# A deformable convolution and a ternary convolution block on one core: the work in front of the loop in another order, with image 0's offsets summed and replicated ahead of its pixels' low parts and their store

## What is computed

```python
x = x + L0(gn(x))    # deformable 3x3 convolution, 128 -> 128 channels
x = x + L1(gn(x))    # two ternary 3x3 convolutions with batch norm, relu(out1 + out2)

# L0, in short
om = conv2d(x, w_off) + b_off                  # 27 channels: 9 row offsets, 9 column offsets, 9 masks
mask = sigmoid(m)
sampled = four corners of x at (base + tap + offset), bilinear, times mask
out = einsum('bckhw,ock->bohw', sampled, weight) + bias
out = group_norm(out, 16 groups) * gamma + beta
```

## Time and profile before

| | us |
|---|---|
| median of 3 runs | 272.83 |
| lowest, highest | 272.41, 274.51 |
| the profiled execution | 272.33 |
| its span in the trace | 270.6 |
| TensorE busy in the span | 244.2 |
| VectorE | 213.6 |
| ScalarE | 171.9 |
| GpSimd | 166.3 |

### The profile page before, as it was taken

The page is one execution under the profiler, slowest core; times in us unless marked ns, Lnnn a source line. Parts: engine busy times, 40 slices in busy tenths (PEclk is TensorE's granted clock), DMA queues, the critical chain, the costliest instruction groups (busy, mean ns, idle before and its releaser), DMA issues.

```text
span 270.6 us, 5607 instructions
## 1 busy us (share of the span) xinstructions
PE 244.2 (90%) x1960; PEld 210.8 (78%) x1960; DVE 213.6 (79%) x473; ACT 171.9 (64%) x364; POOL 166.3 (61%) x217
## 2 busy tenths in 40 slices
PE   6989998999999899998998999899999999999800
PEld 6867666899988799897998888899987776777600
DVE  5599556989888999559979789985588787699493
ACT  2488756989779978877799778757216406630140
POOL 8000899999668788777668987486900601936051
PEclk9999999999999999999999999999999999999965
DMA  7925686544444422333323334300000000000016
GB/s 216 378 69 186 208 263 239 164 146 135 133 140 135 127 95 75 110 114 108 111 79 105 96 131 132 103 30 2 0 0 0 2 1 0 0 0 2 5 54 261
DMA packets 25593, 28.13 MB, mean 104 GB/s; under 512 B 2509, under 2 KB 23613, under 8 KB 25560
## 3 DMA queue, kind: packets, MB, share of 16 engines
q1 hardware_dynamic: 24912, 25.95, 29.3%
q10 hardware_dynamic: 648, 1.76, 1.8%
HBM read 19.87 MB, written 6.78 MB: 99 GB/s over the span
## 4 chain that ended last, share of the span: by engine, by line
PE 64%; DVE 22%; ACT 8%; issue 2%; DMA 1%; DVEq 0%
PE PS L949 13%; PE PS L855 6%; PE PS L741 5%; PE PS L808 5%; PE PS L857 5%; PE PS L856 5%; PE PS L837 5%; DVE slo L1556 5%; PE PS L984 4%; PE PS L838 4%; PE PS L839 4%; DVE vlo L1567 3%; DVE st L1455 3%; ACT vhi L1165 3%; PE PS L767 2%
## 5 line engine op out<-in xcount | busy, mean ns | idle before, releaser
L581 POOL TENSOR_TENSOR vt<-rowm,hat 128x1026 f32<-128x1026 f32 x36 | 70.8, 1966 | 25.9 <-PE PS L817 24.1
L1567 DVE TENSOR_TENSOR vlo<-PS,vhi 128x576 fp32r<-128x576 f32 (+2 forms) x88 | 50.1, 590 | 17.5 <-ACT vhi L1165 17.2
L1165 ACT ACTIVATE vhi<-PS 128x576 fp32r<-128x576 f32 (+2 forms) x88 | 43.8, 523 | 19.1 <-PE PS L839 19.0
L1556 DVE TENSOR_TENSOR slo<-PS,shi 114x512 fp32r<-114x512 f32 (+1 forms) x68 | 43.2, 675 | 6.3 <-ACT shi L1153 6.0
L855 PE MATMUL PS<-vhi,wdhi 128*128 128x256 f32 x144 | 43.4, 301 | 0.8 <-ACT xb L1172 0.7
L837 PE MATMUL PS<-shi,patch 114*128 114x288 f32 (+1 forms) x136 | 42.0, 309 | 1.0 <-DVE vlo L1567 0.6
L857 PE MATMUL PS<-vhi,wdlo 128*128 128x256 f32 x144 | 40.5, 281 | 0.0
L856 PE MATMUL PS<-vlo,wdhi 128*128 128x256 f32 x144 | 40.4, 281 | 0.0
L838 PE MATMUL PS<-slo,patch 114*128 114x288 f32 (+1 forms) x136 | 40.2, 296 | 0.0
L839 PE MATMUL PS<-shi,patch 114*128 114x288 f32 (+1 forms) x136 | 40.0, 294 | 0.0
L1153 ACT ACTIVATE shi<-PS 114x512 fp32r<-114x512 f32 (+1 forms) x68 | 36.7, 592 | 4.9 <-PE PS L808 4.4
(11 more groups left out here) (217 smaller groups left out, 518.0 us busy)
## 6 DMA issues: line engine op xcount, KB each, us to landing
patch<-xt SPq DMA_DIRECT2D x136, 114.0 KB
xt<-xtv SPq DMA_DIRECT2D x4, 1024.0 KB, 6.2
xs<-in_x SPq DMA_DIRECT2D x3, 512.0 KB, 7.5
wraw<-in_L_conv_w SPq DMA_DIRECT2D x2, 576.0 KB, 9.5
out<-xb SPq DMA_DIRECT2D x4, 256.0 KB, 2.6
wd_raw<-in_L_conv_weight ACTq DMA_DIRECT2D x1, 576.0 KB, 6.9
xs<-in_x SPq DMA_DIRECT2D x2, 256.0 KB, 4.1
omr<-omr SPq DMA_DIRECT2D x8, 64.0 KB, 4.5
```

The source lines that it names most:

```text
L581: g.tensor_tensor(vt[:, n % 2, :, :].rearrange("p t (r j) -> p t r j", r=WR), rowm[:, n % 2, :, :].unsqueeze(3).to_broadcast([P, TAPS, WR, ...
L1165: last = a.activation(places(vhi), src, ACT.Copy)
L1556: d.tensor_tensor(lo, src, hi, ALU.subtract).then_inc(slo_ok, 1 if pairs(n) == 2 else 3)
L1567: last = d.tensor_tensor(places(vlo), src, places(vhi), ALU.subtract)
```

## The change

The change moves steps of the work in front of the loop, on every engine:

- SyncE issues `replicate(0)` ahead of `store_pixels(0)`.
- VectorE does half of image 2's statistics earlier, `deformable_lo(2)` ahead of the second `deviation`, then `scale_shift(GN0, 2)`, `offsets(0)`, `offsets(1)` and only then `pixels_lo(0)`. It also makes `xlo` of image 3, behind `offsets(3)` and ahead of `pixels_lo(3)`; `low_parts(3)` on GpSimd is gone.
- ScalarE does `tail(0)` and `tail(1)` ahead of `whole(GN0, 1)`.
- TensorE takes the group mean of images 2 and 3 after the last of six matmuls of `offset_part(1, 0, 0)` instead of after the first, `group_square(GN0, 2)` behind `turn_offsets(0)`, and `turn_image(1)` ahead of `offset_part(1, 0, 1)`.
- The six matmuls of `keep_going` at the start (128 columns, on the identity, after GpSimd made it) give way to nine of 512 columns on a tile of zeros, which can start once VectorE has written the zeros.

```diff
@@ sync
+            replicate(0)
             store_pixels(0)
-            replicate(0)
             sp.wait_ge(zpad_out, 16 * (B + 1))
             store_pixels(1)
@@ gpsimd
-                if n == -4:
-                    low_parts(3)
@@ tensor
-            pe.wait_ge(consts, 1)
-            keep_going(6)
+            zeros = woffT[:, :, :, :].rearrange("p l x c -> p (l x c)")
+            pe.wait_ge(zeroed, 4)
+            for _ in range(9):
+                t.matmul(PS[0:STACK, 5, :], zeros[:, 0:STACK], zeros[:, 0:BIG], start=True, stop=True)
...
             SUMS = {(0, 0, 0): ((group_mean, 1, (2, 0)),), (0, 1, 0): ((group_square, 1, (0, 0)),),
-                    (1, 0, 0): ((group_mean, 2, (0, 0)), (group_square, 2, (2, 1)))}
+                    (1, 0, 0): ((group_mean, 2, (2, 1)),)}
...
             turn_offsets(0)
+            group_square(GN0, 2)
+            turn_image(1)
             offset_part(1, 0, 1)
-            turn_image(1)
@@ scalar
             heads(GN0, 1)
-            whole(GN0, 1)
             tail(0)
             tail(1)
+            whole(GN0, 1)
@@ vector
             image_stats(GN0, 1)
+            dve.wait_ge(x_in[2], 16)
+            half_stats(GN0, 2, 0)
             deviation(GN0, 1)
...
-            dve.wait_ge(x_in[2], 16)
-            image_stats(GN0, 2, last=False)
+            image_stats(GN0, 2, last=False, halves=(1,))
             deformable_lo(0)
             dve.wait_ge(x_in[3], 16)
             image_stats(GN0, 3)
             deformable_lo(1)
+            dve.wait_ge(pads, 11)
+            deformable_lo(2)
             deviation(GN0, 2)
             tails(GN0, 1)
...
-            dve.wait_ge(pads, 11)
-            deformable_lo(2)
-            pixels_lo(0)
+            scale_shift(GN0, 2)
             offsets(0)
             offsets(1)
-            scale_shift(GN0, 2)
+            pixels_lo(0)
             whole_late(2)
...
             offsets(3)
+            dve.wait_ge(xhi_ok, B)
+            dve.wait_ge(xn_late, 2)
+            d.tensor_tensor(inner(xlo, B - 1), square(plain(B - 1)), inner(xhi, B - 1), ALU.subtract).then_inc(xlo_last, 1)
             pixels_lo(3)
```

More of the change, by code:

```diff
@@ L181, in build @@
             sem(n) for n in ("gn_in", "gn_mean", "gn_dev", "gn_msq", "gn_var", "gn_std", "gn_ok"))
-        xhi_top, xhi_ok, xlo_ok, xlo_pool, xlo_first, xn_ok, xn_late = (
-            sem(n) for n in ("xhi_top", "xhi_ok", "xlo_ok", "xlo_pool", "xlo_first", "xn_ok", "xn_late"))
+        xhi_top, xhi_ok, xlo_ok, xlo_last, xlo_first, xn_ok, xn_late = (
+            sem(n) for n in ("xhi_top", "xhi_ok", "xlo_ok", "xlo_last", "xlo_first", "xn_ok", "xn_late"))
         xt_mm, xthi_ok, xtlo_ok, zpad_out = sem("xt_mm"), sem("xthi_ok"), sem("xtlo_ok"), sem("zpad_out")
@@ L546, in point_edges @@
                 return m.bitcast(F32).rearrange("p (r x) -> p r x", x=PW)[:, :, 0:PW:PW - 1]
[L548 to L552, removed]
             def distances(n):
@@ L728, in offset_part @@
                 elif b == 3:
-                    pe.wait_ge(xlo_pool, 1)
+                    pe.wait_ge(xlo_last, 1)
                 else:
```

## The result

The change made the kernel slower, by more than the range allowed:

| | before | after |
|---|---|---|
| median of 8 runs, us | 273.24 | 276.11 |
| lowest, highest | 272.41, 274.51 | 274.92, 279.36 |
| ratio, 95% interval | | 1.010 (1.0071 to 1.0129) |
| the profiled execution | 272.33 | 275.92 |
| its span | 270.6 | 274.2 |

The account below looks back on a forecast made before the run. The prediction took the loop as bound by TensorE's own work, so only its start could move: 272.33 + 0.6 = 272.9 for the profiled execution, 273.4 by the runs' median. It said 273.1, range 271.0 to 274.8.

Parts of the forecast that it names:

- The loop is bound by TensorE and a shift of its start comes out at the end.: Main loop: TensorE busy 19.58 of 20 us, so a shift of its start comes out nearly one to one.
- The gain on the mask, 0.4 (0.0 to 0.7).: Image 0's offsets, ahead of the loop: SyncE begins `replicate(0)` near 22.87 instead of 23.27.
- `replicate(0)`: issue 2.5, landing 2.1.: Image 0's four transfers on SyncE: 2.5 us to issue with no store ahead, the last landing 2.1 after issue.
- The store of image 0: issued at 25.4, landing 4.8 later.: Store behind the four transfers: lands near 30.2, so `pixels_hi(2)` starts at 30.3, 2.8 us later.
- The rival in which the two stores land together: Stores of images 0 and 1 share transfer engines; image 0's lands at 33.3, time 276.0; chance 0.05.
- The steps behind the store and the loop's start at 36.0.: From `pixels_hi(2)` to `pixels_lo(3)`: 5.7 us of steps, so `turn_pairs_out(0)` begins near 36.0 instead of 35.40.
- Image 3's low part on VectorE: Ahead of the loop: 1.23 us, run during 1.3 us of ScalarE's `masks(1)` and `pixels_hi(3)`, costing nothing.
- The patches: First chunks' fetches 2.9 us later but closely in time, cost nothing; as rival, 1 to 2 us, 274 to 275, chance 0.05.
- The first matmuls: Kernel start: nine of 512 columns take 3.8 us, cost the transposes up to 0.6 us, taken as nothing.
- the early clock as a rival: Nine first matmuls raise TensorE's clock early, saving 1.5 us up to the mask; 271.4 to 271.9; chance 0.26.
- the prediction's own argument against the rival: Before the loop: only single matmuls from 6 us until 8.81, so a clock won early may be lost before it pays.
- 0.6 predicted: Loop start: `turn_pairs_out(0)` 0.6 us later, from 35.40 to near 36.0, with ends of -0.2 to +1.6.

Follow-up runs that it names:

- two: The changed kernel with image 0's store back ahead of `replicate(0)`; 275.14 us, ratio 1.0043 to the kernel before.
- four: The changed kernel with the six old matmuls of 128 columns at the start instead of nine of 512; 276.00 us, ratio 1.0100 to the kernel before.
- three: The changed kernel with image 3's low part back on GpSimd; 276.36 us, ratio 1.0104 to the kernel before.
- five: The changed kernel with SyncE's fetches of chunks 0 to 3 in one piece, ahead of store 2, `replicate(1)` and store 3; 275.44 us, ratio 1.0062.
- six: The changed kernel with image 3's low part still on VectorE but ahead of `pixels_lo(2)`; 277.70 us, ratio 1.0170 to the kernel before.
- nine: The kernel before with only the fetches of chunks 0 to 3 in one piece, ahead of the later stores; 273.52 us, ratio 0.9997.
- one: The kernel before with only image 0's store moved behind `replicate(0)`; 277.51 us, ratio 1.0148.
- seven: The kernel before with image 0's store behind `replicate(0)` and the fetches of chunks 0 to 3 in one piece; 275.27 us, ratio 1.0079.

## Why the prediction was wrong

It said 273.1, within 271.0 to 274.8, and gave 0.09 to slower; it was 276.1. Step by step:

*The loop is bound by TensorE and a shift of its start comes out at the end.* Only half right. The shift of 2.06 did come out, but in the loop's first seven chunks the fetches set a pace of their own, and there the loop is not indifferent.

*The gain on the mask, 0.4 (0.0 to 0.7).* It was -0.1: `replicate(0)` at 23.38, before 23.27. TensorE did reach `turn_offsets(0)` earlier, at 19.11 (predicted 18.9, before 20.10); the root came at 20.94 (20.6), and the sums began at 22.16 (21.8). That the scale and the root take most of TensorE's gain was right; in fact they take all of it. The prediction's own rows give 0.3 and not 0.4 (22.06 to 21.8), and measured are 0.2 more in front of `turn_offsets(0)` and 0.1 more from there to the root. The clock is not the reason: in two it rose at 12.53, no later than in the kernel before, and the sums began at 22.08, before at 22.06. But the clock moves this moment in either order. I had treated its rise as fixed; over the kernels here it lies between 11.3 and 15.0. Where it rose at 11.3 (four), `replicate(0)` began at 22.64; in three, five, six and nine, where it rose at 14.3 or later, at 24.03 to 24.29.

*`replicate(0)`: issue 2.5, landing 2.1.* Measured 2.54 and 2.0.

*The store of image 0: issued at 25.4, landing 4.8 later.* Issued at 25.96 and landed 4.8 later, at 30.76; the store of image 1 landed at 34.02. The rival in which the two stores land together is refuted.

*The steps behind the store and the loop's start at 36.0.* Without image 3's low part the chain was right: I had 36.0 - 22.87 = 13.13 from `replicate(0)` to the loop, and one, three, six and seven all show 13.13. That the hundredths agree is luck, since the terms were rounded to a tenth.

*Image 3's low part on VectorE: "1.23 ... and costs nothing".* **This step failed.** It cost 0.88 of the path, shown by three and by six. The prediction counted 1.23 beside 1.3 of ScalarE's work, which would have covered it, and didn't look at what GpSimd does at that moment: `vt`, for 1.96. With 2.27 the cover is too short by 1.0, about that much.

*The patches: "I take nothing for it".* **This step failed, and is the largest.** It cost 1.5 us in the changed kernel's profile, and in one 2.5 and a fall of the clock behind it. The prediction had priced this as a rival, 1 to 2 us in all and 274 to 275, and gave it 0.05. Chunk 3's four fetches were out by 50.2, where I had 49.0, and the last patch landed at 55.48, where I had 51 to 53 from the small transfers of `replicate(0)`. In the kernel before, the last patch of chunk 3 was there at 52.45 and its sampling began at 52.97, so there was 0.5 us to spare; chunks 5 and 6 had 0.1 and 0.2. The change made the landing 3.0 later and the loop 2.06.

What the patches stand behind is the store of image 3, issued at 45.38. The trace has sixteen counts of the semaphore for a store, all at its end; for a patch it has one right behind the issue and only six at the end. Ten counts of that store came by 49.79, the other six only from 51.38 to 52.02. So it looks as if a patch went through six of the transfer engines, and the store was late on these six, behind chunk 2's patches (the last landed at 49.29); the counts don't name the engines. The first count of a finished patch of chunk 3 follows at 52.28, the last at 55.48: 3.5 us for four patches behind the store, with a DMA share of 0.40 from 51 to 53. Two windows of the changed kernel show the rates (from 30 the store of image 1 and the first patches; from 33 patches, with the end of that store until about 33.5; from 34 to 37, patches alone, it is 142 GB/s at a DMA share of 0.41):

```profile
30.00:33.00 3.00, 3.00 (x17) 1.00 1.05 345
33.00:37.00 4.00, 2.56 (x10) 1.00 0.42 136
```

The store moves at 345 GB/s, patches at 136 to 142. By that four patches of 114 KB, 456 KB, take 3.2 to 3.4 us. So the queue doesn't recover fast, since a chunk takes TensorE 4.1 us (28.8 us for seven, from the first line of `turn_last_out` above) and its patches 3.2 to 3.4. Five and seven test this: with chunk 3's fetch ahead of the stores of images 2 and 3, the waits at chunk 3 go, though the fetches begin no earlier.

The prediction passed over the DMA share, 0.41 in the earlier trace rows. It looks like a path with room, but patches alone don't go above it. The Trainium skill ("DMA: Bandwidth & Descriptors", Why a DMA increments its semaphore by 16 and not by 1) gives the reading: a transfer is spread over the largest number of transfer engines, up to 16, that divides the outermost size of both its sides. A patch is 6 rows of 19 pixels in memory and 114 partitions in the core's own memory, so that number is 6. The six late counts of a patch agree, and so does the share, since 6 of 16 is 0.38 and the windows show 0.41 to 0.42; no run here changed the shape of a patch.

*The first matmuls: nothing, if the clock doesn't change; the early clock as a rival.* Both half came: the clock rose early (1.40 us for the transposes instead of 2.19) and was lost before the offsets, as the prediction's own argument against the rival said. Four, with the old first matmuls, has the time of the changed kernel, so the net effect is none that can be measured.

The sum with measured terms: 0.6 predicted, + 0.5 for the mask, + 0.9 for image 3's low part, + 1.5 for the patches, is 3.5; the profile shows 3.6. The medians show 2.9 with an interval of 1.9 to 3.5.

What stays open: medians and profiles don't always rank the kernels alike (six against three), and by the medians the order of the fetches gives back less than by the profiles (0.4 in five, 1.8 in seven). The clock's rise and its falls in the loop may be part of that; I can read them in a profile but did not control them. Also not tried: a patch shape that spreads over more transfer engines.

## What to carry to other kernels

When a change delays a transfer, follow every transfer queued behind it until the queue has caught up, and compute the catching up from the rate that the same transfers show in a window of their own; the share of busy DMA engines doesn't tell that a path is full. A step that moves to an engine "with time to spare" is costed against what the neighbour engine does in that very microsecond, too. And where two chains feed a loop, shortening the one that isn't last only turns into a wait at the other, so a control that relieves the second chain alone (five, seven, nine) settles in one run what the first can't.

## What the runs showed of the hardware that was not expected

- VectorE and GpSimd hold each other up for whole instructions, in both directions: VectorE's 1.22 us low part took 2.27 beside `vt`, GpSimd's 0.28 us step took 1.26 beside the low part; in two, where VectorE was first, its step took 1.22 and `vt` 2.90 instead of 1.96. In each case the later one pays about the rest of the earlier one. A low part of pixels, which has one of its two inputs in `PS`, is not held up: 1.21 at 36.03, beside GpSimd's steps. The Trainium skill ("SBUF — State Buffer", Who interferes with whom) describes the port pair that they share as an exclusive lock, and the rows agree.
- TensorE's granted clock can fall in the middle of a busy loop. It fell in four of the twelve kernels' profiles (one, two, four, nine), each time for 3.4 us, and each fall cost 0.7 to 1.7 us. In one it came right behind a wait of 2.48 us, and the two together cost 4.2; in two it came 3 us after a wait of 1.63. In four and nine, where it came at 45, the longest wait in the 5 us ahead of it was 0.31 us, which the kernel before has too, without a fall. So what sets off a fall is open.
- The moment at which the clock rises to 2.4 GHz for good differed between kernels with the same first matmuls by up to 3 us (11.3 in four has the same ones as 14.3 in nine; two and three have the new ones, 12.5 and 15.0), and `replicate(0)` moved with it, from 22.64 to 24.29 where it stands ahead of the store.
- A transfer can leave most of the transfer engines idle and still hold up its queue: a patch has six counts at its end where a store has sixteen, patches alone move 142 GB/s at a DMA share of 0.41 where stores move 345 at 1.05, and behind patches the last six counts of a store came up to 2.2 us after the first ten (52.02 and 49.79).
